# The end of an eight-batch graph network kernel, reordered: the last attention's norm first, the work of the batch before as filler

## The reference

```python
y = (adj @ x + x) @ w0 + b0;  x1 = LN(x + y / max(norm(y), 1e-12))            # layer 0
A = exp(8 * tanh((x1 @ q) @ (x1 @ k).T / sqrt(128) / 8)) * adj
x2 = LN(x1 + (A / sum(A)) @ x1 @ v)                                            # layer 1, attention
res = si[:, None] + sj[None, :] + adj * w_r + g_b                              # si = x2 @ w_i, sj = x2 @ w_j
x3 = LN(x2 + (res @ x2) @ w2 + b2)                                             # layer 2
L = eye - D^-1/2 adj D^-1/2;  T2 = 2 L L - eye
out = LN(x3 + relu(x3 @ W0 + L @ x3 @ W1 + T2 @ x3 @ W2 + b3))                  # layer 3, Chebyshev
```

## Time and profile before

| | us |
|---|---|
| median of 3 runs (lowest, highest) | 730.44 (730.24, 732.1) |
| profiled execution, its own time | 728.46 |
| its span, first to last instruction | 726.3 |
| TensorE busy | 644.0 (89%) |
| VectorE busy | 615.4 (85%) |
| ScalarE busy | 383.9 (53%) |
| GpSimd busy | 70.5 (10%) |

### The profile page before, as it was taken

The page is one execution under the profiler, slowest core; times in us unless marked ns, Lnnn a source line. Parts: engine busy times, 40 slices in busy tenths (PEclk is TensorE's granted clock), DMA queues, the critical chain, the costliest instruction groups (busy, mean ns, idle before and its releaser), DMA issues.

```text
span 726.3 us, 17483 instructions
## 1 busy us (share of the span) xinstructions
PE 644.0 (89%) x7478; PEld 487.4 (67%) x7478; DVE 615.4 (85%) x1562; ACT 383.9 (53%) x525; POOL 70.5 (10%) x49
## 2 busy tenths in 40 slices
PE   4846955899999999999999999999999999949894
PEld 3533632566876688668866687668866886636894
DVE  3889898998989898989989898989898997886625
ACT  4829906763459154934486355915493448541302
POOL 0020001000200120011200120012001120020002
PEclk9969987999999999999999999999999999969998
DMA  8010001000100020001000020002000100001002
GB/s 270 38 29 1 1 1 30 1 1 1 32 2 2 1 60 2 1 3 36 25 1 2 1 60 2 2 1 60 2 1 2 31 2 1 2 0 30 3 2 59
DMA packets 20013, 14.54 MB, mean 20 GB/s; under 512 B 864, under 2 KB 18912, under 8 KB 19936
## 3 DMA queue, kind: packets, MB, share of 16 engines
q1 hardware_dynamic: 18816, 12.91, 5.9%
q10 hardware_dynamic: 1120, 0.52, 0.3%
HBM read 9.24 MB, written 4.19 MB: 18 GB/s over the span
## 4 chain that ended last, share of the span: by engine, by line
PE 48%; DVE 34%; ACT 9%; issue 4%; POOL 3%; DMA 1%; SPq 1%; ACTq 0%; DVEq 0%
PE r L1099 10%; PE r L1101 10%; PE r L1100 10%; DVE p_lo L775 5%; DVE att L770 4%; DVE stats L506 4%; ACT att L375 3%; POOL small L240 3%; DVE x L928 2%; PE m L1099 2%; PE m L1101 2%; PE m L1100 2%; DVE x L545 2%; PE av L1213 2%; PE av L1216 2%
## 5 line engine op out<-in xcount | busy, mean ns | idle before, releaser
L240 POOL TENSOR_TENSOR small<-small,minus_half 128x8 f32<-128x8 f32 x39 | 66.1, 1700 | 605.5 <-DVE small L528 482.1
L375 ACT ACTIVATE att<-r,coef 128x1024 f32<-128x1024 f32 x64 | 70.4, 1101 | 49.8 <-PE r L1101 49.2
L1213 PE MATMUL av<-vhi,p_hi 128*128 128x129 f16 x512 | 89.7, 220 | 6.8 <-DVE p_lo L775 6.4
L1216 PE MATMUL av<-vhs,p_lo 128*128 128x129 f16 x512 | 89.5, 220 | 0.0
L1215 PE MATMUL av<-vlo,p_hi 128*128 128x128 f16 x512 | 89.5, 219 | 0.0
L770 DVE TENSOR_TENSOR att<-att,adjT 128x1024 f32<-128x1024 f32 x64 | 77.9, 1218 | 10.9 <-ACT att L377 10.9
L775 DVE SCALAR_TENSOR_TENSOR p_lo<-p_hi,att 128x1024 f16<-128x1024 f16 x64 | 77.8, 1217 | 0.0
L1099 PE MATMUL r<-gr,lap 128*128 128x128 f16 x448 | 75.9, 219 | 0.0
L1101 PE MATMUL r<-gr,lap 128*128 128x128 f16 x448 | 75.8, 219 | 0.0
L1100 PE MATMUL r<-gr,lap 128*128 128x128 f16 x448 | 75.8, 219 | 0.0
L1099 PE MATMUL r<-xq,lap 128*128 128x128 f16 x448 | 75.4, 219 | 0.0
(11 more groups left out here) (294 smaller groups left out, 1921.4 us busy)
## 6 DMA issues: line engine op xcount, KB each, us to landing
x<-in_x SPq DMA_DIRECT2D x8, 512.0 KB, 4.2
lap<-in_adj SPq DMA_DIRECT2D x8, 512.0 KB, 8.7
out<-outb SPq DMA_DIRECT2D x7, 512.0 KB, 3.4
out<-att SPq DMA_DIRECT2D x1, 384.0 KB, 2.8
b_bc<-in_L_gnn_bias SPq DMA_DIRECT2D x3, 64.0 KB, 6.5
x<-in_L_gnn_weight ACTq DMA_DIRECT2D x1, 192.0 KB, 7.3
out<-att SPq DMA_DIRECT2D x1, 128.0 KB, 2.7
x<-in_L_gnn_q ACTq DMA_DIRECT2D x1, 64.0 KB, 4.0
```

The source lines that it names most:

```text
L240: return nc.gpsimd.tensor_tensor(dst, src, minus_half[:], ALU.pow)
L375: nc.scalar.activation(att[:, s], (r1, r0)[t % 2][:], ACT.Tanh, scale=c_tanh).then_inc(S["th"], 1)
L1213: mm(acc, p_hi[:, s, chunk(j)], vhi[:, t, 0:D + 1], start=(t == 0 and j % 3 == 0), stop=False, skip_group_check=True)
L1216: l_ = mm(acc, p_lo[:, s, chunk(j)], vhs[:, t, 0:D + 1], start=False, stop=(t == C - 1), skip_group_check=True)
```

## The change

TensorE, last attention loop: parts 4 to 7 of batch 6's adjacency product move behind attend 7. Then follow: w2 product of 6, the whole adjacency product of 7 into r1 (two banks, so no wait between the halves), `sum_x2`, transposes of 6, `sums_w2`, w2 product of 7, r, p and u of 6, the Laplacian of 6 but its last chunk, transposes of 7, the last chunk. VectorE: `row_sums`, residuals and norm 1 of batch 7 first; the rest of batch 6 and batch 5's last statistics behind. ScalarE and GpSimd are ordered to match. No arithmetic is added or removed.

```diff
@@ gpsimd
+            norm_root(1, B - 1)
             norm_root(2, B - 2)
             norm_root(3, B - 3)
-            norm_root(1, B - 1)
             norm_root(2, B - 1)
@@ scalar
+            norm(1, B - 1, x2, V_CHUNKS)
             y2_hi(B - 2, 1)
+            copy_x2(B - 1)
             norm(2, B - 2, x3, V_CHUNKS)
+            act.wait_ge(S["p2_mm"], B - 1)
+            for h in range(2):
+                y2_hi(B - 1, h)
             act.wait_ge(S["o_mm"], 2 * (B - 2))
             for h in range(2):
                 x3t_hi(z_all, B - 2, h)
-            norm(1, B - 1, x2, V_CHUNKS)
-            copy_x2(B - 1)
             for h in range(2):
                 r_hi(z_all, B - 2, h)
...
             p_copy(z_all, B - 2)
             norm(3, B - 3, outb, 0)
-            act.wait_ge(S["p2_mm"], B - 1)
-            for h in range(2):
-                y2_hi(B - 1, h)
-            q_hi(z_all, B - 2, 0)
             norm(2, B - 1, z_end.x3, V_CHUNKS)
             for h in range(2):
                 x3t_hi(z_end, B - 1, h)
+            q_hi(z_all, B - 2, 0)
             q_hi(z_all, B - 2, 1)
@@ vector, the new order whole
+            row_sums(B - 1)
+            for j in range(C):
+                l_ = attention_residual(j)
+            l_.then_inc(S["e1a"], 1)
+            dve.wait_ge(S["e1a"], B)
+            ln_begin(1, B - 1, x2)
             l2_ch = Count(dve, S["l2_c"], B - 2, L2_LINKS)
             l2_ch.n = 2
             l2_row(l2_ch, z_all)
+            ln_shift(1, B - 1)
+            ln_norm(1, B - 1, x2)
+            y2_lo(B - 2, 1)
+            x2_lo(B - 1)
             l2_end(l2_ch, z_all, B - 2)
             ln_begin(2, B - 2, x3)
+            sj_ch = Count(dve, S["sj_c"], B - 1, 5)
+            for k_ in range(2):
+                sj_step(sj_ch, B - 1, k_)
+            ln_shift(2, B - 2)
             ln_norm(2, B - 2, x3)
+            for k_ in range(2, 4):
+                sj_step(sj_ch, B - 1, k_)
+            y2_lo(B - 1, 0)
+            y2_lo(B - 1, 1)
+            sums_read(B - 1, av[:, 2])
+            sums(B - 1)
             for h in range(2):
                 x3t_lo(z_all, B - 2, h)
             l2_ch = Count(dve, S["l2_c"], B - 1, L2_LINKS)
             l2_read(l2_ch, B - 1, av[:, 2])
             dve.wait_ge(S["pl"], C * B)
             l2_rank_one(l2_ch, z_end)
+            for h in range(2):
+                r_lo(z_all, B - 2, h)
             l2_row(l2_ch, z_end)
             l2_end(l2_ch, z_end, B - 1)
+            dve.wait_ge(S["f_c"], B - 2)
+            ln_stats(3, B - 3, outb)
+            ln_arg(3, B - 3)
             ln_begin(2, B - 1, z_end.x3)
+            ln_shift(3, B - 3)
+            u_part(z_all, B - 2)
             ln_shift(2, B - 1)
             ln_norm(2, B - 1, z_end.x3)
+            q_part(z_all, B - 2, 0)
             q_part(z_all, B - 2, 1)
             for h in range(2):
                 x3t_lo(z_end, B - 1, h)
+            q_lo(z_all, B - 2, 0)
             q_lo(z_all, B - 2, 1)
@@ tensor, last attention loop
-                if prev:
+                if prev and nxt:
                     adj_x2(C - AHEAD - 1)
                 for t in range(C - AHEAD, C):
                     if cur:
                         attend(t)
-                    if prev and t == C - AHEAD:
+                    if prev and nxt and t == C - AHEAD:
                         for part in range(t, C):
+                            adj_x2(part)
+                    if prev and not nxt and t == C - 1:
+                        for part in range(C - AHEAD - 1, C):
                             adj_x2(part)
@@ tensor, the end, the new order whole
             project(r0, yT, w2s[:, 0], w2s[:, 1]).then_inc(S["p2_mm"], 1)
+            pe.wait_ge(S["e1b"], B)
+            for part in range(8):
+                adj_x2_part(B - 1, part, r1)
+            pe.wait_ge(S["sj_c"], 5 * B)
+            sum_x2(av[:, 2])
             x3_t(z_all, B - 2)
+            sums_w2(av[:, 2], B - 1)
+            pe.wait_ge(S["y2_lo"], 2 * B)
+            project(r1, yT, w2s[:, 0], w2s[:, 1]).then_inc(S["p2_mm"], 1)
             pe.wait_ge(S["e1a"], B)
             r_product(z_all, B - 2)
             p_product(z_all)
             u_product(z_all, B - 2)
             pe.wait_ge(S["p_cp"], B - 1)
+            apply_laplacian(r0, gr, 0, C // 2).then_inc(S["t_mm"], 1)
+            apply_laplacian(r0, gr, C // 2, C - 1)
             x3_t(z_end, B - 1)
+            apply_laplacian(r0, gr, C - 1, C).then_inc(S["t_mm"], 1)
             pe.wait_ge(S["u_ok"], B - 1)
             r_product(z_end, B - 1)
```

More of the change, by code:

```diff
@@ L327, in y2_hi @@
                 act.wait_ge(S["y2_mm"], 2 * b + h + 1)
-                copy(yT[:, 0, half(h)], m7[:], Y2_DOWN).then_inc(S["y2_hi"], 1)
+                copy(yT[:, 0, half(h)], r1[:, half(h)] if is_first(b, B - 1) else m7[:], Y2_DOWN).then_inc(S["y2_hi"], 1)
             def x3t_hi(z, b, h):
@@ L663, in y2_lo @@
             def y2_lo(b, h):
-                split_lo(yT[:, 1, half(h)], m7[:], Y2_DOWN, yT[:, 0, half(h)], "y2", 2 * b + h + 1)
+                src = r1[:, half(h)] if is_first(b, B - 1) else m7[:]
+                split_lo(yT[:, 1, half(h)], src, Y2_DOWN, yT[:, 0, half(h)], "y2", 2 * b + h + 1)
             def sums_read(b, src):
@@ L986, in _ @@
             iterations(dve, body)
-            y2_lo(B - 2, 1)
-            dve.wait_ge(S["f_c"], B - 2)
-            ln_stats(3, B - 3, outb)
+            row_sums(B - 1)
[4 more added lines that the diff above has]
+            ln_begin(1, B - 1, x2)
             l2_ch = Count(dve, S["l2_c"], B - 2, L2_LINKS)
@@ L993, in _ @@
             l2_row(l2_ch, z_all)
+            ln_shift(1, B - 1)
+            ln_norm(1, B - 1, x2)
+            y2_lo(B - 2, 1)
+            x2_lo(B - 1)
             l2_end(l2_ch, z_all, B - 2)
             ln_begin(2, B - 2, x3)
[L996 to L1002, removed]
-            ln_norm(2, B - 2, x3)
-            dve.wait_ge(S["e1a"], B)
-            ln_begin(1, B - 1, x2)
+            sj_ch = Count(dve, S["sj_c"], B - 1, 5)
+            for k_ in range(2):
+                sj_step(sj_ch, B - 1, k_)
+            ln_shift(2, B - 2)
+            ln_norm(2, B - 2, x3)
+            for k_ in range(2, 4):
[4 more added lines that the diff above has]
+            sums(B - 1)
             for h in range(2):
                 x3t_lo(z_all, B - 2, h)
[L1008 to L1021, removed]
             l2_ch = Count(dve, S["l2_c"], B - 1, L2_LINKS)
@@ L1025, in _ @@
             l2_rank_one(l2_ch, z_end)
-            y2_lo(B - 1, 1)
+            for h in range(2):
+                r_lo(z_all, B - 2, h)
             l2_row(l2_ch, z_end)
             l2_end(l2_ch, z_end, B - 1)
+            dve.wait_ge(S["f_c"], B - 2)
+            ln_stats(3, B - 3, outb)
+            ln_arg(3, B - 3)
             ln_begin(2, B - 1, z_end.x3)
-            q_part(z_all, B - 2, 0)
+            ln_shift(3, B - 3)
+            u_part(z_all, B - 2)
             ln_shift(2, B - 1)
             ln_norm(2, B - 1, z_end.x3)
+            q_part(z_all, B - 2, 0)
             q_part(z_all, B - 2, 1)
-            q_lo(z_all, B - 2, 0)
             for h in range(2):
                 x3t_lo(z_end, B - 1, h)
+            q_lo(z_all, B - 2, 0)
             q_lo(z_all, B - 2, 1)
@@ L1139, in adj_x0, with adj_x2_part @@
                     l_.then_inc(S["y0_mm"], 1)
-            def adj_x2_part(b, part):
+            def adj_x2_part(b, part, dst=None):
                 h, m0 = part // 4, 2 * (part % 4)
-                if part == 4:
+                if part == 4 and dst is None:
                     pe.wait_ge(S["y2_lo"], 2 * b + 1)
+                dst = m7[:] if dst is None else dst[:, half(h)]
                 for m in range(m0, m0 + 2):
-                    l_ = split_product(m7[:], x2s[:, 0, m], x2s[:, 1, m], a_hi[:, m, half(h)], a_lo[:, m, half(h)],
+                    l_ = split_product(dst, x2s[:, 0, m], x2s[:, 1, m], a_hi[:, m, half(h)], a_lo[:, m, half(h)],
                                        m == 0, m == C - 1)
@@ L1396, in _ @@
             p_product(z_all)
-            pe.wait_ge(S["e1b"], B)
-            for part in range(4):
-                adj_x2_part(B - 1, part)
             u_product(z_all, B - 2)
             pe.wait_ge(S["p_cp"], B - 1)
[L1402 to L1413, removed]
+            apply_laplacian(r0, gr, 0, C // 2).then_inc(S["t_mm"], 1)
+            apply_laplacian(r0, gr, C // 2, C - 1)
             x3_t(z_end, B - 1)
+            apply_laplacian(r0, gr, C - 1, C).then_inc(S["t_mm"], 1)
             pe.wait_ge(S["u_ok"], B - 1)
```

## The result

The changed kernel takes 728.68 us (median of 20 runs, 727.33 to 729.79), the kernel before, run beside it, 730.91 us (20 runs, 729.14 to 732.1). The ratio is 0.9968 (95% interval 0.9963 to 0.9974): 2.2 us, 0.3%, faster. The forecast was 727.0, 3.4 us faster.

A forecast was written before the change was run, and what follows sets the result against it. TensorE bounds the end, VectorE's chain the stretch before: its last norm comes 5.9 us earlier (3.0 from earlier attention), but late small things leave batch 7's last layer 3.4 earlier. 730.44 - 3.4 = 727.0 us; range 725.4 to 729.7.

The forecast's parts named there:

- Step 1: Last attention loop: with the matmuls ahead of the last attend blocks moved behind them, attention's result comes 3.0 us earlier.
- Step 2: Head of the end, from row sums through batch 7's norm 1: w2 product starts at 640.46, after 5.0 us idle, not 9.1.
- Step 3: TensorE's clock after that stop: low for 3.5 us from the restart, w2 product 2.6 us, 1.45 us on the path.
- the holding clock: Rival: TensorE's clock stays full through the 5 us stop before the w2 product; gain 4.9 us, 725.5; chance 0.09.
- the long one: Rival: clock stays low 6.8 us after the restart at the w2 product; gain 1.8 us, 728.6; chance 0.13.
- Step 4: VectorE's chain from l2_end to the last norm: 29.4 us without real wait, the norm ending 5.9 us earlier.
- unseen wait: Rival: a wait of 2 us or more in VectorE's chain eats the gain; about 730; chance 0.06.
- filler: TensorE's work beside VectorE's chain, before batch 7's transposes: 1 us short of the chain, so VectorE is the bound.
- Step 5: Before batch 7's last layer: late norm chunks, last laplacian chunk and queued x3t_lo; TensorE stands 1.0, 0.7 and 1.55 us.
- The second fall of the clock: Rival: short stops between 672 and 677 us lower TensorE's clock again, costing 2.1 us; gain 1.3, 729.1; chance 0.09.
- the slower rival: A clock fall at 674.7 lasts 13.6 us, slowing the last layer and first long laplacian; 2.1 us slower, 732.5; chance 0.05.
- the forecast's own: Range of the main case: clock back 1 to 5.5 us after the restart, medians moving 0.7 us; chance 0.58.

## Why the forecast was right, and 0.9 us too good

**Step 1** held: reciprocals at 23.20 for 23.15. The loop with its old order confirms the size: 2.95 us for the 3.0 of the step.

**Step 2** is the mis-sized term. It priced the root at 1.64 us "covered for 1.2 by l2_row"; it took 2.54, since that cover is itself what holds GpSimd. All that follows is later by the same amount: the w2 product by 1.08, l2_end by 1.05, the last norm's end by 0.94, the last layer by 0.95. So 3.4 us became 2.5 between the marks. The Trainium skill says it in "SBUF — State Buffer", section "SBUF: two separate sides": VectorE and GpSimd share a pair of SBUF ports under an exclusive lock that lasts for a whole instruction, and a VectorE operation with two SBUF inputs (or in a two-port mode, which is not looked into here) keeps it from a GpSimd operation that reads SBUF. The roots shown here agree, with 1.64 us beside statistics, 2.01 beside 0.68 us of such an operation and 2.54 beside 1.22. In the other direction the traces do not bear the lock out: VectorE's second half of 0.69 us was not held while the root ran. I had taken GpSimd's price from the nearest row without asking what VectorE did beside that row, and l2_row moved over a root is just the case that the section describes.

**Step 3** held within 0.6 us: back 4.1 us after the restart where I took 3.5 from the earlier trace rows; the w2 product took 2.53 us for 2.6. That the first of the two is so close is in part luck: restarts without longer gaps took 3.5, 4.1, 4.6 and 4.9 us in these traces, and the one in the head, the same code, 3.5 us in one execution and 6.7 in the other. Of the rivals, the holding clock did not come (5.8 us of stop, it fell 3.1 us after the last work), and neither did the long one (6.8). The long one's time, 728.6, is the measured one, but its mechanism is not: the trace has 4.1 us, and the missing time is the root's. With unread products in the stop, the holding clock was worth 1.28 us; the forecast had laid out 1.5 for it (4.9 in place of 3.4).

**Step 4** held: from l2_end's start to the last norm's end 29.34 us, where the forecast's two marks lie 29.45 apart. No unseen wait of 2 us. Its filler was 1.0 us short by the forecast and 0.77 by the trace. The root under sj step 0 was long as well (2.56), but sj steps 0 and 1 cover it to within about 0.1 us.

**Step 5** held: stops of 0.77, 0.46 and 1.47 us for 1.0, 0.7 and 1.55. VectorE's q_part is the cause of the last, as the experiment with x3t_lo ahead of it shows. The second half of the transposes waits for ScalarE's three chunks (676.21 for 1.25 us), which stand behind batch 5's eight, as laid out:

```profile
676.21 1.25 ACT L315 ACTIVATE att<-att,small 128x128 f32<-128x128 f32 x3
```

From the first product of the last layer on, everything is as before: 25.46 us before and 25.45 after to the last output.

**The second fall of the clock** did not come, and so neither did the slower rival: the clock stays at 1.00 through the three short stops. What the Trainium skill tells of one kernel in "TensorE: Matmul & The Clock Gate", section "A second HAM failure mode: psum-queue depth-cycling", that frequent short stops make the clock swing, did not come for these three. The prediction read the low clock at 132.0 as following "a stop of only 0.99 us"; in the trace of before that stop is one of five between 120.7 and 132 us (the others 1.41, 0.62, 0.22 and 0.76), and TensorE was at work for 7.32 of the 11 us from 121 on. In the changed kernel it was at work for 6.30 of the 9 us from 672 on, and the clock held, so the rows leave open what it takes.

**The median.** The measured 728.68 lies in the whole range (725.4 to 729.7) but 0.5 us above the forecast's own, 726.1 to 728.2. 727.0 was 3.4 under the 730.44 of three runs; over twenty the kernel before has 730.91. Of the 1.7 us between forecast and result, 0.5 are this and 0.95 the root; 0.3 are the difference between the marks (2.5) and the medians (2.2), within what these can tell.

## What to carry to other kernels

A price taken from a row holds for the company that the row had: before an instruction of GpSimd is priced, look at what VectorE ran beside the row, and what it will run beside the new place. Work put under a wait for GpSimd should have one input in SBUF, or one of two in PSUM: with statistics there in place of an add, and two other small edits, the end gained 4.2 us more (1.6 of it by the statistics), as against 2.5 for the whole change. And a reordering is priced as a whole: of the two halves of this one, one costs 5.2 us alone, the other gains nothing (0.7 us of cost by the marks, none by the medians), and together they gain 2.5.

## What the runs showed of the hardware

- A GpSimd tensor_tensor of 128x8 takes 1.64 us, 2.54 with a VectorE add of 128x1024 that started 0.17 us before it, 2.01 with one of 128x512, and 2.01 with two of these in a row. A VectorE instruction of 1.28 us with one of its two inputs in PSUM did not lengthen it (1.64), and the root did not lengthen a VectorE add of 128x512 that started beside it (0.69).
- TensorE's clock fell 3.1 us after the last work and was back 4.1 us after the restart; with l2_row behind the norm (4.8 us of stop) 4.9 us after it; with the old order in the loop (11 us of stop) back at 651.9, 4.6 us after it; and in the head, after stops of 13.1 us, 3.5 us after it in one execution and 6.7 in another. Products that nobody reads, put into the stop, kept it at the full level.
- The head, the same code in both kernels, took 2.7 us longer in one profiled execution than in the other, nearly all of it in the first 123 us.
